# Bias of the graph attention added by the projection, and the division of the sums shared by two engines

## What is computed

```python
def gat_conv(x, src, dst, w, a_src, a_dst, bias):
    h = (x @ w).reshape(N, H, HD)
    s = jnp.sum(h * a_src, axis=-1)
    d = jnp.sum(h * a_dst, axis=-1)
    e = jax.nn.leaky_relu(s[src] + d[dst], negative_slope=0.2)
    m = jax.ops.segment_max(e, dst, num_segments=N)
    ex = jnp.exp(e - m[dst])
    denom = jax.ops.segment_sum(ex, dst, num_segments=N)
    alpha = ex / (denom[dst] + 1e-16)
    msg = h[src] * alpha[:, :, None]
    out = jax.ops.segment_sum(msg, dst, num_segments=N)
    return out.reshape(N, H * HD) + bias
...
h = jax.nn.elu(layer_norm(x @ w_in + b_in, g_in, bt_in))
for i in range(L):
    identity = h
    y = gat_conv(h, src, dst, w_l[i], a_s[i], a_d[i], b_l[i])
    y = jax.nn.elu(y)
    y = layer_norm(y, g_l[i], bt_l[i])
    h = y + identity
```

## Time and profile before

| | |
|---|---|
| median of 3 runs | 7684.07 us (7683.78 to 7686.03) |
| profiled execution | 7691.76 us |
| its span | 7690.0 us |
| busy in the span: PE, VectorE, ScalarE, GpSimd | 70%, 65%, 56%, 51% |
| `gnn_input` | about 145 to 395 us |
| `gat_finish` of layers 0, 1, 2 | about 1675 to 1904, 3138 to 3366, 4611 to 4793 us |

### The profile page before, as it was taken

The page is one execution under the profiler, slowest core; times in us unless marked ns, Lnnn a source line. Parts: engine busy times, 40 slices in busy tenths (PEclk is TensorE's granted clock), DMA queues, the critical chain, the costliest instruction groups (busy, mean ns, idle before and its releaser), DMA issues. The chain is left out here.

```text
span 7690.0 us, 106452 instructions
## 1 busy us (share of the span) xinstructions
PE 5415.3 (70%) x24694; PEld 4030.1 (52%) x24694; DVE 5030.4 (65%) x13781; ACT 4268.1 (56%) x13681; POOL 3924.3 (51%) x3916
## 2 busy tenths in 40 slices
PE   1757777744677777437777750899997888887678
PEld 1634444423455555325555530899994466665335
DVE  5555555666567676756666657777773387778673
ACT  4457777864688888548778773455554422111132
POOL 3276666646767677467666753000000277777322
PEclk7867788876789898768888885999998898887789
DMA  6243333333444444343433333100005644333302
GB/s 169 76 126 103 103 101 104 103 82 122 137 112 113 112 113 111 87 145 108 111 106 108 110 79 109 48 19 20 20 20 184 221 121 123 108 106 99 94 21 74
DMA packets 492760, 774.99 MB, mean 101 GB/s; under 512 B 86759, under 2 KB 368311, under 8 KB 492279
## 3 DMA queue, kind: packets, MB, share of 16 engines
q0 software_dynamic: 168240, 452.12, 21.5%
q1 hardware_dynamic: 324183, 319.65, 13.2%
HBM read 634.42 MB, written 146.27 MB: 102 GB/s over the span
## 5 line engine op out<-in xcount | busy, mean ns | idle before, releaser
L1679 POOL DMA_INDIRECT gm_got<-scratch_feat,keep_src_tab x2520 | 2503.7, 994 | 1091.7 <-issue 633.0
L1885 ACT ACTIVATE gm_got<-gm_got 128x64 f32<-128x64 f32 x10080 | 2453.1, 335 | 4.7 <-DVE gm_got L1813 4.7
L1933 PE MATMUL gm_bank<-gm_got,gm_onehot 128*128 128x264 f32 x5040 | 1844.7, 479 | 773.7 <-DVE gm_onehot L1836 429.2
L1933 PEld LDWEIGHTS gm_bank<-gm_got,gm_onehot 128*128 128x128 f32 x5040 | 1028.4, 228 | 1250.8 <-issue 647.9
L1830 DVE TENSOR_TENSOR gat_acc<-gat_acc,gm_bank 128x264 f32 x2520 | 1074.6, 426 | 706.3 <-PE gm_bank L1933 436.9
L1014 POOL DMA_INDIRECT mix1a_got<-scratch_rel_feat,layer_rel_tab x240 | 244.7, 1020 | 1397.7 <-issue 1396.7
L1014 POOL DMA_INDIRECT mix1b_got<-scratch_rel_feat,layer_rel_tab x600 | 608.6, 1014 | 190.8 <-issue 187.5
L1064 PE MATMUL mix1b_m_bank<-mix1b_got,mix1b_onehot 128*128 128x256 f32 x1200 | 398.0, 468 | 159.3 <-DVE layer_acc L1041 122.0
L1836 DVE TENSOR_TENSOR gm_onehot<-keep_iota_row,keep_dst_tab 128x896 f32<-128x896 f32 x360 | 385.7, 1080 | 27.7 <-PE gm_bank L1933 24.9
L1064 PEld LDWEIGHTS mix1b_m_bank<-mix1b_got,mix1b_onehot 128*128 128x128 f32 x1200 | 252.0, 228 | 269.6 <-DVE mix1b_onehot L1021 171.3
L3017 ACT ACTIVATE moe_h<-moe_first,moe_shift,moe_gain 128x256 f32<-128x256 f32 x400 | 203.7, 559 | 253.7 <-PE moe_first L3058 253.7
(11 more groups left out here) (559 smaller groups left out, 12232.8 us busy)
## 6 DMA issues: line engine op xcount, KB each, us to landing
scratch_rel_feat<-rel_out SPq DMA_DIRECT2D x50, 1024.0 KB, 5.5
gm_got<-scratch_feat,keep_src_tab POOLq DMA_INDIRECT x2520, 2.8
gm_flags<-scratch_flags SPq DMA_DIRECT2D x90, 280.0 KB
gf_feat<-scratch_feat SPq DMA_DIRECT2D x75, 256.0 KB, 4.1
gf_old<-scratch_hidden SPq DMA_DIRECT2D x75, 256.0 KB, 4.7
scratch_hidden<-gf_h SPq DMA_DIRECT2D x75, 256.0 KB, 3.6
scratch_feat<-gf_row SPq DMA_DIRECT2D x50, 260.0 KB, 3.5
gm_x<-scratch_x SPq DMA_DIRECT2D x50, 256.0 KB
```

The costliest lines, as they stand in the source:

```text
L1679: nc.gpsimd.indirect_dma_start(out=got[:, place // GROUPS, place % GROUPS * GROUP + j, 0:GAT_ROW], out_offset=None, in_=dram["feat"][layer ...
L1885: last = nc.scalar.activation(rows, rows, ACT.Copy, scale=got[:, b, i, D + h:D + h + 1])
L1933: nc.tensor.matmul(bank[i % BANKS][:, 0:GAT_SUM], onehot[:, i % HOTS, :], got[:, v[1] % B, i, :], start=True, stop=True).then_inc(s_sum, 1)
```

## The change

The bias leaves `gat_finish` and is added by PE when rows are projected. Because the weights alpha sum to one, a bias in every projected row comes out once in the weighted sum; the scores are still computed from rows without it. PE does it with one more product per tile, a row of ones by the row `b_l`, into the same accumulation. `Projection` serves `gnn_input` and layers 0 and 1, so the new products are in these three. GpSimd's addition and the semaphore between its two steps go. The division of a pair's second tile moves from VectorE to ScalarE, as one activation with a scale per row for each head, at the start of ScalarE's "sums"; VectorE's addition waits for it (s_y1).

```diff
@@ Projection
+        self.b, self.ones = sb("b_l", [1, D]), sb("p_ones", [1, P])
+        self.s_ones = sem("p_ones")
...
+        sp.dma_start(self.b[:, :], self.io["L0_gnn_b_l"][self.layer].rearrange("(o n) -> o n", o=1)).then_inc(self.s_w, 16)
...
-        dve.wait_ge(self.s_w, 48)
+        nc.vector.memset(self.ones[:, :], 1.0).then_inc(self.s_ones, 1)
+        dve.wait_ge(self.s_w, 64)
...
     def start_pe(self, pe):
+        pe.wait_ge(self.s_w, 64)
+        pe.wait_ge(self.s_ones, 1)
         pe.wait_ge(self.s_wa, 1)
...
     def project_pe(self, pe, u, n):
-        project_pair(self.nc, bank, self.ht[:, u], self.w)
+        for i in range(PAIR):
+            out = bank[:, i * D:(i + 1) * D]
+            for a in range(HALVES):
+                self.nc.tensor.matmul(out, self.ht[:, u, a, i * P:(i + 1) * P], self.w[:, a, :], start=(a == 0), stop=False)
+            self.nc.tensor.matmul(out, self.ones[:, :], self.b[:, :], start=False, stop=True)
@@ gat_finish
-        rows = {n: sb(n, [P, D]) for n in ("b_l", "g_l", "bt_l")}
+        rows = {n: sb(n, [P, D]) for n in ("g_l", "bt_l")}
...
             def _(pool):
-                pool.wait_ge(s_w, 48)
                 pool.wait_ge(s_factors, 2)
...
-                            last.then_inc(s_self, 1)
-                            pool.wait_ge(s_self, n)
-                            nc.gpsimd.tensor_tensor(feat[:, u], feat[:, u], both(rows["b_l"][:, :]), ALU.add).then_inc(s_sum, 1)
+                            last.then_inc(s_sum, 1)
...
             def _(dve):
                             dve.wait_ge(s_h, n)
-                            for i in range(PAIR):
-                                t = tile_at(r, u, i)
-                                last = nc.vector.tensor_tensor(one_tile(y[:, u, i]), one_tile(acc[:, t, 0:D].rearrange("p t d -> p (t d)")),
-                                                               spread(of_edges, t), ALU.mult)
-                            last.then_inc(s_y, 1)
+                            t = tile_at(r, u, 0)
+                            nc.vector.tensor_tensor(one_tile(y[:, u, 0]), one_tile(acc[:, t, 0:D].rearrange("p t d -> p (t d)")),
+                                                    spread(of_edges, t), ALU.mult).then_inc(s_y, 1)
                         for u, n in slots(r):
                             dve.wait_ge(s_y, n)
+                            dve.wait_ge(s_y1, n)
                             dve.wait_ge(s_sum, n)
...
             def _(act):
+                act.wait_ge(s_factors, 2)
...
                     if name == "sums":
+                        for u, n in slots(r):
+                            act.wait_ge(s_h, n)
+                            t = tile_at(r, u, 1)
+                            for h_ in range(H):
+                                cols = slice(h_ * GAT_DIM, (h_ + 1) * GAT_DIM)
+                                last = nc.scalar.activation(y[:, u, 1, cols], acc[:, t, cols].rearrange("p t d -> p (t d)"), ACT.Copy,
+                                                            scale=of_edges[:, t, h_:h_ + 1].rearrange("p t h -> p (t h)"))
+                            last.then_inc(s_y1, 1)
                         for u, n in slots(r):
                             act.wait_ge(s_yb, n + UNROLL)
                             elu.parts(nc, u, n, y[:, u])
```

More of the change, by code:

```diff
@@ L1976, in gat_finish @@
         project = None if last_layer else Projection(nc, space, io, dram, keep, gathers, layer + 1, scores, 7)
-        s_w, s_sum, s_y, s_yb, s_elu, s_ya, s_h, s_dve, s_fall, s_factors, s_stored, s_self = (
-            sem(n) for n in ("s_w", "s_sum", "s_y", "s_yb", "s_elu", "s_ya", "s_h", "s_dve", "s_fall", "s_factors", "s_stored",
-                             "s_self"))
+        s_w, s_sum, s_y, s_y1, s_yb, s_elu, s_ya, s_h, s_dve, s_fall, s_factors, s_stored = (
+            sem(n) for n in ("s_w", "s_sum", "s_y", "s_y1", "s_yb", "s_elu", "s_ya", "s_h", "s_dve", "s_fall", "s_factors", "s_stored"))
         s_feat, s_old, s_sent = space.sems("s_feat", UNROLL), space.sems("s_old", UNROLL), space.sems("s_sent", UNROLL)
@@ L2068, in _ @@
                 dve.sem_inc(s_factors, 1)
-                dve.wait_ge(s_w, 48)
+                dve.wait_ge(s_w, 32)
                 if project:
```

## The result

The changed kernel is slower: 7788.18 us (median of 4 runs, 7781.65 to 7806.95) against 7683.97 us for the kernel before (7683.78 to 7686.03), a ratio of 1.0136 with a 95% interval of 1.0123 to 1.0148. The forecast was 7655 us, the range 7637 to 7686. The profiled execution took 7781.65 us with a span of 7779.9 us, 89.9 us more than the span before.

A forecast was written before the change was run, and what follows sets the result against it. No engine was taken to bound the changed stages throughout; a round's chain through VectorE and ScalarE, disturbed by GpSimd, did. 2 x (13.5 - 7.8) + 21.9 - 4.1 - 0.4 = 28.8 us saved, giving 7655 us, range 7637 to 7686.

The forecast's parts named there:

- rivals on ScalarE's pitch: ScalarE's divisions in gat_finish at 0.37 us each, no gain, 7686 us (chance 0.14); or 0.45 each, slower, 7705 (0.08).
- A: Part of a gat_finish round from h's start (first: first division) to next elu total; layer 0 forecast 11.2, then 17.8 us.
- B's: Parts of gat_finish rounds from elu total's start to h's start; layer 0 forecast 17.6, 15.9, 19.9, 19.9, 15.2 us.
- In rounds inside gat_finish this is hidden: Layers 0 and 1's inner rounds: PE's extra 7.8 us costs nothing, projections ending some 26 us after h, scores read at 33.
- cover: Inner rounds of gat_finish: time between PE's projections ending, some 26 us after h's start, and VectorE reading scores at 33.
- I take it to keep the higher clock: gnn_input's inner rounds, fifth projection slot: PE hardly stands, so 4.2 instead of 5.33 us, 3.7 saved over four rounds.
- The bound of 16.6: gnn_input: most it could lose if the fifth slot stayed at half clock, 8.8 us plus 7.8 for the last round.
- unused relief: Rival: layers 0 and 1 give 0, input stage loses 16 us with PE at half clock, layer 2 keeps some 20; 7680, chance 0.14.
- Layer 2's end: gat_finish without projection: ScalarE free for divisions and GpSimd's slots shorter, 21.9 us saved in all.
- all else keeps its instructions: Everything outside the input stage and the three layer ends, message stages included, was put at no change.
- disturbed rounds: Layers 0 and 1's ends: rounds where GpSimd slows VectorE, 23.9 us from h to elu total; a gain of 6.1 forecast.
- undisturbed rounds: Layers 0 and 1's ends: rounds without GpSimd's interference, 14.4 us from h to elu total; a loss of 3.4 forecast.

The follow-up runs named there:

- k5: Changed kernel with idle increments placing layers 1 and 2's message loops, bias product over 128 rows instead of one: 7615.97 us, ratio 0.9873 to the kernel before.
- k1: Changed kernel plus 22 and 106 idle semaphore increments on VectorE in layers 0's and 1's ends: 8786.93 us, ratio 1.0022 to the kernel before.
- k2: Kernel before plus 106 idle semaphore increments on VectorE in layer 0's end, nothing of the change: 8748.57 us, ratio 0.9981.
- k8: Kernel before plus 89, 41 and 97 idle increments on VectorE in the input stage and layers 0's and 1's ends: 7658.56 us, ratio 0.9928.
- k15: Kernel before plus 53, 77 and 97 idle increments, so layer 0's message loop is placed too: 8686.36 us, ratio 0.9921.
- k6: As k5, but each full-row bias product made twice with 0.5 in place of 1: 7625.82 us, ratio 0.9885 to the kernel before.
- k7: Changed kernel with placed loops as in k1, a pair's two one-row bias products beside each other: 7623.97 us, ratio 0.9887 to the kernel before.
- k11: As k5, but both divisions of a pair stay on VectorE: 8608.32 us, ratio 0.9914 to the kernel before.
- k14: Changed kernel with bias over 128 rows, ScalarE's division in layer 2 alone, all three message loops placed: 8639.42 us, ratio 0.9862 to the kernel before.

## Why the prediction was wrong

**The prices of single instructions were right.** ScalarE's twenty divisions take what the earlier trace rows said, 0.24 us each:

```profile
1761.45 4.88 ACT L2131 ACTIVATE gf_y<-gat_acc,gf_of_edges 128x64 f32 x20
```

Both rivals on ScalarE's pitch are out. A slot with two bias products takes 4.26 us at the high clock where 4.2 was forecast, and the last slots of the input stage and of layer 0's end stand that far apart; in layer 1's end the clock fell among them.

**VectorE's stretches were right where PE kept up.** In layer 0 the first A was 10.7 us (forecast 11.2), the second 17.9 (17.8); the B's were 16.9, 15.7, 18.4, 18.6 and 15.2 (17.6, 15.9, 19.9, 19.9 and 15.2). The later A's were 19.0, 20.2 and 22.7 instead of 17.8: L774 waits for ScalarE, and ScalarE for transposes that PE makes late.

**The step that failed first** is "In rounds inside gat_finish this is hidden". Its 26 us fit PE's 17.7 of a round before (1722.09 to 1739.79) with the 7.8 of the new products added at an unchanged clock, against 33 us until the scores are read. With the lone one-row products the clock fell in the middle of the projections, the slot went to 8.01 us, PE ended the round after 36.2 us, and the 7 us of cover were gone. The last round of layer 0's end then cost 16.8 us more instead of 7.8, since it had to wait for the one before, and layer 1's 26.7 more. k5 shows the step by itself: the same count of products over 128 rows leaves the cover whole. There the time from the first division to the last h fell by 18.7 us (forecast 13.5), the last round cost 4.1 us more, and layers 0 and 1's ends save 14 us each, against the 5.7 forecast.

**The input stage** was the larger miss, +50 against +4. "I take it to keep the higher clock" was said of the fifth slot; in truth the slots from the second or third on lost it as well, which made VectorE wait 49 us more for the scores. The bound of 16.6 priced only the fifth at half clock, so it was no bound. The rival "unused relief" put PE at half clock too, but in that one slot. The mechanism of this loss, PE's clock brought down by the new products themselves, stood in none of the cases.

**Layer 2's end** was right: 24 us saved, 21.9 forecast.

**The message stages** were put at nothing because their instructions are the same ("all else keeps its instructions"), and the text named a move of theirs as what would make it wrong. They measured 50 us more. A change of code length in one stage moved VectorE's loop in the next: the loop of layer 1 from 2568 to 2550, a bad place, and that of layer 2 from 3774 to 3737, a good one. That placement moves the packets and these stages is shown (k1, k2, k8, k15 and their repeats). That it makes the whole of 84 us in a 7.7 ms session is not shown. For it speak 1230 to 1238 us in k5, k6 and k7 with good places and 1314 in the changed kernel with a bad one. Against it, the pairs measured in sessions of 8.7 ms give 33 to 45 us, and of the waits that grew in the changed kernel they repeat the one ahead of the loop but not the 26 us ahead of L1859. The cause of the rest is open; the changed kernel with well placed loops has no run in a 7.7 ms session.

**ScalarE's part** was credited with a gain in disturbed rounds of layers 0 and 1. It has next to none there. GpSimd's relief alone brings the disturbed A's from 23.9 to 18.6 us (k11, k14), and with ScalarE's division they are 17.9 and 17.2 in k5: gains of 0.7 and 1.4, not of 6.1. In the undisturbed rounds it lost 3.5 and 2.9, with 3.4 forecast. So the relief alone shortens these ends by 15 to 18 us, bias products over 128 rows included, and the division on ScalarE takes 3.5 to 4 of them back. The price of ScalarE's part was right; what was wrong was to set it against A's that the other part had already shortened.

## What to carry to other kernels

Before adding work beside a busy engine, ask what the new instructions do to that engine's own clock, not only what they take: here two biases by lone one-row products cost 0.8 us each and came with half the clock for much of what stood around them, while the same products over 128 rows took 0.4 each and left the clock high. Compare stages that the change didn't touch as well. If one of them moved, look at the packets that load instructions before looking for a story in the data; here a few idle instructions were worth 0.7% of the run (k8), about as much as the repaired change itself (k14 beside k15, 0.5%).

## What the runs showed of the hardware

- Two lone one-row products in a slot of 128-row ones: the granted clock fell from 2.4 to 1.2 GHz while PE had no pause at all (1770.87 in layer 0's end), and the mean was 0.59 against 0.77 with more work over full rows. It was 0.71 with one lone one-row product in a slot and 0.74 with two side by side.
- Lone one-row products of 256 fp32 columns lengthened a slot by 0.82 us each, two side by side by 0.63 each, one over 128 rows by 0.43.
- A loop of 340 or 364 instructions on VectorE brings 4 to 5 more packets of instructions in each turn or none, by its start modulo 128 instructions; a wait of 2.7 to 3.0 us then stands ahead of its first instruction in most turns, and the message stages of layers 1 and 2 take 26 to 53 us longer where kernels of one session can be compared. In the changed kernel layer 1's took 84 us longer; what made it more than in those pairs isn't known.
- What made the message stages 200 us longer in four of the five sessions isn't known. The same chip ran both kinds.
